# Attention on one Trainium2 core: the last GpSimd block of a batch is weighed in the second step of the next batch

## What is computed

```
q = (x @ Wq.T).reshape(d, n, h)
k = (x @ Wk.T).reshape(d, n, h)
v = (x @ Wv.T).reshape(d, n, h)
a = jnp.einsum('dnh,dmh->dnm', q, k) * scale
a = a + spatial_encoding + edge_encoding
a = jax.nn.softmax(a, axis=2)
out = jnp.einsum('dnm,dmh->dnh', a, v)
```

## Time and profile before

| | |
|---|---|
| median of 3 runs | 11981.39 us (11977.12 to 12008.36) |
| the profiled execution: its own time | 11991.02 us |
| its span from first to last instruction | 11989.2 us |
| granted TensorE clock, mean of the span | 0.971 |
| busy shares PE, PEld, DVE, ACT, POOL | 93%, 43%, 83%, 88%, 68% |
| the attention's four chunks | from 844 us to 11308 us of the span |

### The profile page before, as it was taken

How to read it: one execution, slowest core, us unless ns; L and a number is a source line. 1 busy time by engine, 2 the same in 40 slices (tenths; PEclk the granted TensorE clock), 3 DMA queues, 4 the chain that set the end, 5 groups by cost and what they waited for, 6 DMA issues and landing times. The chain is left out here.

```text
span 11989.2 us, 378481 instructions
## 1 busy us (share of the span) xinstructions
PE 11097.4 (93%) x138570; PEld 5158.3 (43%) x138570; DVE 9919.4 (83%) x10282; ACT 10586.3 (88%) x9570; POOL 8128.2 (68%) x4114
## 2 busy tenths in 40 slices
PE   4759999999999999999899999999899999999877
PEld 4524444444444444444333333434333343433473
DVE  6358888888878888888788888888788888888728
ACT  3249999999989999999899999999899999999705
POOL 0017777777767777777677777777677777777500
PEclk7979999999999999999999999999999999999988
DMA  8783333333343333333433333333433333333354
GB/s 314 230 238 59 59 57 58 59 57 58 56 88 57 59 58 57 59 58 56 89 53 53 53 53 53 54 53 54 86 53 53 53 53 54 54 53 53 62 174 154
DMA packets 432589, 943.40 MB, mean 79 GB/s; under 512 B 100727, under 2 KB 349438, under 8 KB 381470
## 3 DMA queue, kind: packets, MB, share of 16 engines
q1 hardware_dynamic: 432508, 942.28, 39.8%
HBM read 799.88 MB, written 142.00 MB: 79 GB/s over the span
## 5 line engine op out<-in xcount | busy, mean ns | idle before, releaser
L1014 DVE SCALAR_TENSOR_TENSOR a_probs<-ps,a_adj 128x768 f32<-128x768 f32 (+1 forms) x9216 | 8983.0, 1020 | 1345.2 <-PE ps L907 1224.0
L989 POOL TENSOR_TENSOR a_pool_probs<-a_pool_probs,a_adj 128x768 f32<-128x768 f32 (+1 forms) x4096 | 8111.7, 1980 | 2362.8 <-ACT a_pool_probs L964 2362.8
L969 ACT ACTIVATE a_probs<-a_probs 128x1536 f32<-128x1536 f32 (+3 forms) x5120 | 7347.6, 1458 | 223.7 <-DVE a_probs L1014 193.0
L907 PE MATMUL ps<-a_q,a_k 34*128 34x512 f32 (+2 forms) x26624 | 4993.0, 412 | 415.2 <-DVE a_probs L1014 258.0
L924 PE MATMUL ps<-a_probs,a_v 128*9 128x192 f32 (+1 forms) x73728 | 4212.3, 341 | 6.1 <-ACT a_probs L969 4.0
L964 ACT ACTIVATE a_pool_probs<-ps 128x768 f32<-128x768 f32 (+1 forms) x4096 | 3530.0, 862 | 56.3 <-PE ps L907 35.0
L907 PEld LDWEIGHTS ps<-a_q,a_k 34*128 34x128 f32 x26624 | 2207.6, 185 | 3134.7 <-DVE a_probs L1014 1174.4
L924 PEld LDWEIGHTS ps<-a_probs,a_v 128*9 128x9 f32 x73728 | 1739.4, 90 | 1750.6 <-ACT a_probs L969 621.8
L924 PE MATMUL ps<-a_pool_probs,a_v 128*9 128x192 f32 (+1 forms) x32768 | 2219.0, 343 | 0.0
L924 PEld LDWEIGHTS ps<-a_pool_probs,a_v 128*9 128x9 f32 x32768 | 488.7, 88 | 1226.7 <-issue 1222.8
L126 ACT ACTIVATE g_rstd<-g_stat 128x26 f32<-128x26 f32 x2 | 0.5, 226 | 434.8 <-DVE g_stat L117 434.8
(11 more groups left out here) (181 smaller groups left out, 2075.4 us busy)
## 6 DMA issues: line engine op xcount, KB each, us to landing
a_k<-k_parts SPq DMA_DIRECT2D x2048, 208.0 KB
a_v<-v_ext SPq DMA_DIRECT2D x512, 117.0 KB
adj_t<-tr SPq DMA_DIRECT2D x26, 1664.0 KB, 6.4
g0tile<-adj_t SPq DMA_DIRECT2D x26, 1664.0 KB, 6.9
g2tile<-adj_t SPq DMA_DIRECT2D x26, 1664.0 KB, 6.9
nat<-in_adj SPq DMA_DIRECT2D x25, 1663.5 KB, 10.5
e_nat<-in_adj SPq DMA_DIRECT2D x25, 1663.5 KB, 6.8
a_q<-q_parts SPq DMA_DIRECT2D x2048, 16.0 KB
```

Of the source, the lines that this page charges most:

```text
L907: ins = nc.tensor.matmul(ps[:, slot + begin:slot + end], kt[row:row + SCORE_ROWS, P * j:P * (j + 1)].bitcast(F32R), qt[row:row + SCORE_ROW ...
L969: nc.scalar.activation(both, both, ACT.Exp, scale=2.0).then_inc(sums_exped, 1)
L989: nc.gpsimd.tensor_tensor(probs(k)[:, :, :], probs(k)[:, :, :], adj_c[:, :, j, :], ALU.mult).then_inc(multiplied, 1)
L1014: v.scalar_tensor_tensor(out=probs(k), in0=score(j).rearrange("p (i q) -> p i q", q=P), scalar=SCALE / 2, in1=adj_c[:, :, j, :], op0=ALU.m ...
```

## The change

`weighed_at` loses its `min`, so that block 23 is weighed in step 27, which is step 1 of the next batch, behind scores 5. For the second batch of a turn that step lies in the next turn. So `turn` now weighs, in its first four steps, what the turn before has left (`weigh_at[units + k]`, with block numbers less `units`, so negative ones: batch -1, the other accumulator). The first turn of a chunk (`begin`) has nothing left to it and is written out ahead of the loop, which runs one turn less; the last (`final`) gets four more steps, in which only block 23 is weighed. `last_weighed` becomes block 23.

```
-        return b * BLOCKS + (min(j + POOL_LAG, BLOCKS - 1) if by_pool[j] else sets[set_of[j]][-1])
-
-    weigh_at = [[k for k in range(units) if weighed_at(k) == at] for at in range(units)]
-    first_weighed, *_, last_weighed = (k for ks in weigh_at[:BLOCKS] for k in ks)
+        return b * BLOCKS + (j + POOL_LAG if by_pool[j] else sets[set_of[j]][-1])
+
+    in_order = sorted(range(BLOCKS), key=lambda j: (weighed_at(j), j))
+    first_weighed, last_weighed = in_order[0], in_order[-1]
+    weigh_at = [[k for k in range(units) if weighed_at(k) == at] for at in range(units + POOL_LAG)]
...
-            def turn(batch, pair, c, final):
-
-                for k in range(units):
+            def turn(batch, pair, c, begin, final):
+
+                for k in range(units + POOL_LAG if final else units):
                     ahead = k + ahead_by
-                    if ahead < units or not final:
+                    if ahead < units or (k < units and not final):
...
+                    if k < POOL_LAG and not begin:
+                        for u in weigh_at[units + k]:
+                            weigh(u - units, batch, c)
                     for u in weigh_at[k]:
                         weigh(u, batch, c)
...
-                with pe.Fori(0, turns - 1) as t:
-                    turn((c * turns + t) * 2, c * turns + t, c, False)
-                turn(c * BATCHES + (BATCHES - 2), c * turns + (turns - 1), c, True)
+                turn(c * BATCHES, c * turns, c, True, False)
+                with pe.Fori(1, turns - 1) as t:
+                    turn((c * turns + t) * 2, c * turns + t, c, False, False)
+                turn(c * BATCHES + (BATCHES - 2), c * turns + (turns - 1), c, False, True)
```

## The result

| | before | with the change |
|---|---|---|
| median of 12 runs each | 11984.68 us (11976.3 to 12043.6) | 11920.33 us (11880.5 to 11968.6) |
| the profiled execution: own time, span | 11991.02, 11989.2 us | 11880.51, 11878.7 us |
| PE, ACT busy | 93%, 88% | 94%, 89% |

The ratio of the medians is 0.9941, with a 95% interval of 0.9924 to 0.9958: faster by 64 us. The forecast was 11886 us and -95 us; the two profiled executions differ by 110 us.

The account below looks back on a forecast made before the run. Attention bounds the kernel, with ACT busy 88% and idle for DVE before exp of (3,5), behind PE's order. Gains of 87 us (7-wide) and 8 us (6-wide) gave 11981.4 - 95 = 11886 us; own range 11860 to 11925, 8 in 10 within 11830 to 11975.

Parts of the forecast that it names:

- no wait for GpSimd: PE's weight loads for GpSimd's blocks: idle for GpSimd only 2.9 us of 1226.7 us, so no such wait to remove.
- The prices: On PE: scores 0.24 us a block plus 0.18 a run; weighings 0.33 (7-wide 0.38) a block plus 0.11 a run.
- The price of an extra pair: Cutting one run of scores and one of weighings on PE costs 0.18 + 0.11 = 0.29 us a batch.
- 7-wide: 7-wide batches: exp of (3,5) 0.37 us earlier, of (6,8) 0.34 earlier; 0.34 x 256 = 87 us won.
- the lateness of 0.03: 7-wide batch: exp of (6,8) could start at 8.75, while ACT would be there at 8.72.
- 6-wide: 6-wide batches: most of the 0.33 us is lost by scores 12; 0.03 x 256 = 8 us won.
- The rest costs nothing.: Later loads, DVE's copy, GpSimd's ring and the first turn written out: below 1 us in all for the extra loop entry.
- The first: Rival: all of the weighing's time won at both widths, 0.37 and 0.33 x 256 = 179 us, 11802 us; chance 0.08.
- The second: Rival: nothing won, ACT's idle 0.31 us moves from (3,5) to (6,8) in 7-wide batches; 11950 to 11990 us; chance 0.14.
- The third: Rival: slower, as the extra switches between scores 5 and 6 bind; +51 us, 12032 us; chance 0.07.
- twice the price: Upper bound for the extra switches on PE, twice 0.29 us: 6-wide loses about 0.25 a batch, 7-wide wins 0.05.
- the last line of the sum: Whole kernel: runs' median taken 9.6 us below the profiled 11991.0 us, so 11981.4 - 95 = 11886 us.

Follow-up runs that it names:

- the code written out: The change's code (first turn ahead of the loop, extra empty steps in the last) with block 23 in its old place, against the kernel before: ratio 0.9994.
- one more pair still: The change with block 23's weighing in two halves, in steps 1 and 3, so two extra pairs of switches: ratio 1.0208 against the kernel before.
- the repeat: The changed kernel run again, unchanged, against the kernel before: median 11932.0 us, ratio 0.9946.
- three orders: The change (7-wide batches 20.92 us apart), block 23 weighed in step 2 instead (20.90), and blocks 23 and 25 both weighed in step 1 (20.94).

## Why the prediction was right, and where it was not

**What bounds the kernel, and no wait for GpSimd.** Right: 2.9 us became 2.6. The change worked through the order on PE alone, and the kernel with block 23 in step 0, which weighs it later too, is slower than before.

**The prices.** 0.24 a block and 0.18 a run of scores, 0.33 (0.38) and 0.11 for weighings. They gave the starts on PE and of these exps to within 0.03 us: forecast and measured, 7-wide, scores 4 at 4.40 and 4.41, weighing of 23 at 5.06 and 5.07, of 0 and 2 at 5.97 and 5.99, scores 7 at 6.84 and 6.86, exp of (3,5) at 6.31 and 6.30, of (6,8) at 8.75 and 8.76; 6-wide, scores 7 at 8.61 and 8.64, (6,8) at 10.37 and 10.40, the weighing of 4 at 11.68 and 11.70. The price of an extra pair, 0.29, was measured as 0.30 and 0.31 with block 23 in step 0.

**7-wide.** Forecast 0.34, measured 0.32. Exp of (9,11) comes at 11.16, where 11.13 was forecast. ACT's wait fell to 6.7 us and not only to 10 to 25: exp of (6,8) starts 0.05 ahead of the end of the record before it, where it had been 0.10, so the lateness of 0.03 that was forecast is there, but no row counts it as a wait. **6-wide.** Forecast 0.03, measured 0.03, for the stated reason: the add of 8 waits for scores 8, scores 12 for the add of 9. The wait before (3,5) fell from 0.42 to 0.29, and exp of (6,8) starts 0.12 behind the end of exp of 7, as forecast in kind. Sum 95, measured 90 in the batches and 94 in the chunks.

**"The rest costs nothing."** Shown for the code written out (0.9994). The later loads cost nothing either: PE's waits for tiles are the four at the starts of chunks.

**Rivals.** The first (all of the weighing's time won, 11802 us) is out: the 6-wide batch won 0.03 of 0.33. The busy share of PE's weight loads, 43%, said nothing of it: in this batch PE has no gap where it matters, and 0.58 us more work on it cost 0.61. The Trainium skill's advice to judge TensorE's headroom by that share (Perfetto Trace Analysis, Identifying the Most-Contended Engine, which names MFU, the share of its peak FLOPs, beside it) is not borne out in the 6-wide batch; in the 7-wide one ACT, which that way of judging makes the busiest of the four engines, is the one that bounds it. The Trainium skill's rule that a change of tiling mode drains TensorE (TensorEngine Tiling (Array Packing), Key Properties) fits the price of the extra pair, though no run shows that scores and weighings are two modes or that the drain is what is paid for. The second is out: the 7-wide batch won 0.32. The third did not come about, since the price of the pair, 0.30 and 0.31, stayed under the 0.32 from which it was to decide in the 6-wide batch. Its mechanism is there all the same: with one more pair still, the batches lengthened by 0.61 and 0.66. For twice the price I had put a loss of 0.25 in the 6-wide batch and a gain of 0.05 in the 7-wide; measured were losses of 0.58 and 0.34 against before. Half a block in a run of its own costs 0.42 and not 0.28, and the 7-wide batch has no room for it either.

**The step that failed** is the last line of the sum: "the median of the runs is 9.6 us lower, and from it I come to 11981.4 - 95". It took the time outside the steady batches to be the same before and after, and a median of three runs for the level. The runs of either kernel are spread over some 80 to 90 us, for the most part with the time that PE stays at 1.2 GHz, and the runs of the change had the lower mean clock, 0.9680 against 0.9692. So the medians show 64, 61 and 65 us where the batches show 90; at one clock, 0.970, they show 82. Why the clock was lower stays open. The profiled execution of the change happened to be the shortest of its 27 runs, so its 11880.5 us flatters the forecast of 11886. And that the median of 11920.3 lies inside the forecast's own range, 11860 to 11925, is in part luck: the repeat had 11932.0, and the kernel before had 11989.5 to 11992.7 in later series, not 11981.4. The sum was that of the batches, and as such it holds.

## What to carry to other kernels

Where an engine alternates between two kinds of work, count the runs and not only the instructions: moving a piece out of a run costs the price of a switch in each direction (here 0.30 us for the pair), so look first for a place where it joins a run of its kind, and for one where the engine would stand anyway. Follow the step behind the stall that goes until something else is late: the same 0.33 us in front of scores 5 was worth 0.32 at one width and 0.03 at the other. And before medians are compared with a sum from the trace, look at whether the runs differ outside the stretch that was changed.

## What the runs showed that I had not expected

- A run of four short matmul records between two runs of scores takes as long as one of eight: 0.42 and 0.44 us in the 6-wide batch, 0.48 and 0.50 in the 7-wide. For so small a piece the length hardly depends on the work in it.
- After the 22 to 80 us in which PE waits at a chunk's start, it begins at the 1.2 GHz level, and when it comes up to 2.4 GHz differs from one execution of the same kernel to the next although PE is busy throughout: over the first 118 us of attention the mean granted clock was 0.85 in one profile of the change and 0.64 in another. The mean clock goes with most of the spread of this kernel's runs, 11 us for each 0.001.
- In the 7-wide batch three orders end at 20.90 to 20.94 us with ACT busy throughout. What they won, 0.30 to 0.34, is about the 0.31 us that ACT stood idle for DVE before, so that idle time, and not the 0.37 of the weighing, was the limit to start from.
- With block 23 in step 2 the 6-wide batch gained 0.13 us and not 0.33, since scores 6 stood 0.2 us for the slot of block 3. A run of scores can come too early to be of use.
